# Seven block products for the gate of six experts, in place of eight, in an adaLN block of attention and a mixture of experts

## The reference, cut to what matters

```python
h = layernorm(x) * (1 + cb) + sb
weights = router(h)                               # (b, t, 8)
gate = einsum('btd,edf->ebtf', h, Wg)             # 8 experts, d = 256, f = 256
up   = einsum('btd,edf->ebtf', h, Wu)
gate[:2] += einsum('btd,edr,erf->ebtf', h, Ga, Gb)   # r = 64, same for up and down
mid = silu(gate) * up
out = einsum('ebtf,efd->ebtd', mid, Wd)
x = x + gb * einsum('bte,ebtd->btd', weights, out)
```

## Time and profile before

| | |
|---|---|
| median of three runs (lowest, highest) | 808.05 us (807.27, 809.63) |
| the profiled execution, and its span | 808.01 us, 806.3 us |
| PE, PE's weight loads, DVE, ACT, POOL busy in the span | 795.3, 710.1, 507.5, 462.2, 395.0 us |
| HBM traffic over the span | 26 GB/s |

### The profile page before, as it was taken

One profiled execution on the slowest core, in us unless ns is written; L12 is line 12 of the kernel. 1 busy time (PEld: TensorE's weight loads), 2 busy tenths in 40 slices (PEclk: granted clock), 3 DMA queues, 4 the chain that ended last, 5 costly groups with the idle time before them and its releaser, 6 DMA issues.

```text
span 806.3 us, 14755 instructions
## 1 busy us (share of the span) xinstructions
PE 795.3 (99%) x5116; PEld 710.1 (88%) x5116; DVE 507.5 (63%) x1074; ACT 462.2 (57%) x1255; POOL 395.0 (49%) x543
## 2 busy tenths in 40 slices
PE   9899999999999999999999999999999999999997
PEld 8688898999999999999999999899888888888887
DVE  5677676476476566557557658667785454454575
ACT  5777686677577677667767776643343232332322
POOL 3777587486576667567567656120011010110493
PEclk9999999999999999999999999999999999999999
DMA  9200010000000000000000000203010110100002
GB/s 333 103 28 2 1 61 1 1 8 2 0 8 2 1 7 2 2 2 6 1 1 8 1 2 2 79 1 94 38 40 2 40 40 1 40 0 1 1 1 105
DMA packets 8170, 21.53 MB, mean 27 GB/s; under 512 B 1561, under 2 KB 4249, under 8 KB 7969
## 3 DMA queue, kind: packets, MB, share of 16 engines
q1 hardware_dynamic: 7520, 20.51, 7.5%
q10 hardware_dynamic: 576, 0.08, 0.1%
HBM read 18.48 MB, written 2.11 MB: 26 GB/s over the span
## 4 chain that ended last, share of the span: by engine, by line
PE 93%; DVE 2%; POOL 1%; ACT 1%; issue 1%; DMA 1%; ACTq 0%; DVEq 0%; POOLq 0%
PE ps_o L663 14%; PE ps_proj L540 9%; PE ps_proj L542 9%; PE ps_proj L541 9%; PE ps_s L540 7%; PE ps_s L541 7%; PE ps_s L542 7%; PE ps_turn L592 4%; PE ps_y L540 4%; PE ps_y L541 4%; PE ps_y L542 4%; PE ps_turn L610 3%; PE ps_turn L540 2%; PE ps_turn L541 2%; PE ps_turn L542 2%; PE ps_o L542 2%
## 5 line engine op out<-in xcount | busy, mean ns | idle before, releaser
L663 PE MATMUL ps_o<-vaug,probs 128*128 128x129 f32 x1024 | 135.3, 275 | 1.6 <-POOL probs L1654 0.9
L663 PEld LDWEIGHTS ps_o<-vaug,probs 128*128 128x128 f32 x1024 | 129.1, 191 | 8.0 <-POOL probs L1654 1.4
L984 ACT ACTIVATE ps_s<-ps_s,knorm 128x512 f32<-128x512 f32 x128 | 79.1, 657 | 95.7 <-PE ps_s L542 95.5
L1267 DVE RECIPROCAL rden<-ps_o 128x2 f32<-128x2 f32 x128 | 21.8, 170 | 154.0 <-PE ps_o L663 153.9
L1660 POOL TENSOR_TENSOR we_lo<-raw_e,we_hi 128x512 fp32r<-128x512 f32 x22 | 28.4, 1316 | 182.3 <-ACT we_hi L1027 182.3
L1237 DVE TENSOR_TENSOR prod<-ps_proj,cs 128x1024 f32<-128x1024 f32 x76 | 92.5, 1217 | 10.9 <-ACT sq L927 10.9
L1605 POOL TENSOR_TENSOR root<-ssq,powers 128x4 f32<-128x4 f32 x76 | 77.7, 1023 | 27.6 <-ACT sq L927 27.6
L927 ACT ACTIVATE sq<-ps_proj 128x128 f32<-128x128 f32 x304 | 79.9, 278 | 18.2 <-PE ps_proj L542 15.2
L1621 POOL TENSOR_TENSOR prod<-prod 128x512 f32<-128x512 f32 x62 | 80.0, 1290 | 9.9 <-DVE prod L1237 9.9
L540 PE MATMUL ps_proj<-w_hi,h_hi 128*128 128x512 f32 x192 | 83.1, 433 | 0.9 <-DVE w_lo L1180 0.5
L1652 POOL TENSOR_SCALAR_AFFINE_SELECT probs<-probs 128x256 f32<-128x256 f32 x64 | 26.3, 410 | 106.1 <-ACT probs L992 105.8
(11 more groups left out here) (212 smaller groups left out, 2178.1 us busy)
## 6 DMA issues: line engine op xcount, KB each, us to landing
raw_e<-in_we SPq DMA_DIRECT2D x8, 768.0 KB, 4.3
raw_p<-in_wqkv SPq DMA_DIRECT2D x6, 512.0 KB, 8.1
raw_e<-in_wo SPq DMA_DIRECT2D x4, 512.0 KB, 11.6
x_all<-in_x SPq DMA_DIRECT2D x1, 1536.0 KB, 7.0
out<-acc SPq DMA_DIRECT2D x3, 512.0 KB, 2.6
x_all<-in_wmod SPq DMA_DIRECT2D x1, 1024.0 KB, 10.0
gates_a<-gate_rows_dram SPq DMA_DIRECT2D x8, 128.0 KB, 2.9
gates_b<-gate_rows_dram SPq DMA_DIRECT2D x1, 1024.0 KB, 8.0
```

What stands on the lines that cost most here:

```text
L663: mm = pe.matmul(ps_o[:, h * (D + 1):(h + 1) * (D + 1)], probs[:, s % 2, at:at + P], vaug[b % 2][:, k, i // 2, :], start=(h == 0 and k == ...
L984: act.activation(ps_s[:, t, :], ps_s[:, t, :], ACT.Tanh, scale=knorm[:, b % 2, t, i // 2:i // 2 + 1]).then_inc(tanh_done, 1)
```

## The change

For tiles 8 to 31 (`SEVEN = FIRST_OF[2]`) the gate is a 2 x 2 block product: weights A (k by f, blocks of 128 x 128) and tokens B (k by two halves of 256 tokens). In place of eight block products it takes seven, of sums of blocks, in Winograd's form of Strassen's method.

- The sums. POOL makes T1, T2, T3 and -T4 from h2 for each group n (`sums_t`, in place, once), and S1 to S4 from each expert's gate weights (`sums_s`, in place, four 128 x 128 operations, each waiting for the one before). Both are split again: ACT `round_t`, `round_s`; POOL `rest_t`, `rest_s`. `sums_s` comes between `split_e(e, 0)` and `split_e(e, 1)` in POOL's order, `rest_s` after `split_e(e, 2)`; on ACT `round_s` follows the three splits.
- PE per tile: `seven_first(m)` (A11·B11, S2·T2 in one bank, S1·T1, S3·T3 in the other, 12 matmuls of 256 columns), `up_alone(m)` (12 of 512), `down(2m-2)`, `seven_last(m)` (three products, 9 of 256, added on top), `down(2m-1)`. The gate has ps_proj only, up has ps_s only.
- The results are put together outside of PE: ACT `copy_seven` copies both banks to `seven` before `seven_last` adds to them; POOL `sums_seven` makes two sums of 256 columns and from them the last quarter of the gate (semaphores `u_made`, `pair_made`, `last_quarter`); DVE `add_quarters` adds the first of these to the second bank (two quarters, `quarters_added`); ACT `silu_seven` takes the first quarter from PSUM and the other three from SBUF in one instruction of 768 columns.
- Moved: POOL's `rest_of_output(0..3)` goes from behind the loop into it, at the end of m = 25, 26, 27, 28, `last_part(0..2)` to the end of m = 29, 30, 31. The low-rank steps come at m = 5, 6 and 7 (two each) in place of m = 5, 6, 8 and 9.
- Low rank: the factors are loaded twice, on partitions 0 to 63 and 64 to 127 (four DMAs in place of two). `lowA_both` holds A's hi part above its lo part, so that one fp32r matmul over 128 partitions gives (hi + lo)·hi, and a second over 64 gives hi·lo: four matmuls for a step in place of two float32 ones of four records.
- h2 of batches 4 and 5 is kept in DRAM (two DMAs that ACT issues in `h2_head`) and read back by SP after expert 3's weights. SP's load of an expert also waits for `s_split`, since the sums are made in the raw weights. Two scratch tiles of the router move.

```diff
-LOW_STEPS = {NEXT + 1: [0, 1], NEXT + 2: [2], NEXT + 4: [3], NEXT + 5: [4, 5]}
+LOW_STEPS = {NEXT + 1: [0, 1], NEXT + 2: [2, 3], NEXT + 3: [4, 5]}
+SEVEN = FIRST_OF[NL]
...
+            def seven_first(m):
+                e, n = TILES[m]
+                q = m - SEVEN
+                of = blocks(m)
+                if m == FIRST_OF[e]:
+                    pe.wait_ge(we_split, 3 * e - 1)
+                    pe.wait_ge(s_split, e - NL + 1)
+                if m == FIRST_OF[NL] + n:
+                    pe.wait_ge(t_split, 2 * n + 2)
+                if q:
+                    pe.wait_ge(quarter_silu, 2 * q - 1)
+                else:
+                    pe.wait_ge(mid_done, 2 * SEVEN)
+                product_of(ps_proj[:, 0, 0:S], of["A11"], of["B11"], True)
+                product_of(ps_proj[:, 0, S:], of["S2"], of["T2"], False).then_inc(seven_ready, 1)
+                if q:
+                    pe.wait_ge(quarters_added, q)
+                product_of(ps_proj[:, 1, 0:S], of["S1"], of["T1"], True)
+                product_of(ps_proj[:, 1, S:], of["S3"], of["T3"], False).then_inc(seven_ready, 1)
+            def seven_last(m):
+                pe.wait_ge(seven_copied, 2 * q + 1)
+                product_of(ps_proj[:, 0, 0:S], of["A12"], of["B21"], False).then_inc(gu_ready, 1)
+                pe.wait_ge(seven_copied, 2 * q + 2)
+                product_of(ps_proj[:, 1, 0:S], of["S4"], of["B22"], False)
+                product_of(ps_proj[:, 1, S:], of["A22"], of["-T4"], False).then_inc(gu_ready, 1)
+            def up_alone(m):
...
+                for f in range(2):
+                    pe.wait_ge(mid_done, 2 * SEVEN if m == SEVEN else 2 * m - 1 + f)
...
-                    mm = pe.matmul((ps_y[:], ps_turn[:, 0, :])[i % 2][:, k * F:(k + 1) * F], lowA[:, e, m3, k * P:(k + 1) * P],
-                                   lowB[:, e, m3, :], start=(k == 0), stop=True, skip_group_check=True)
+                    pe.matmul(dst, lowA_both[:, e, m3, at], lowB_hi[:, e, m3, :], start=(k == 0), stop=False, skip_group_check=True)
+                    mm = pe.matmul(dst, lowA_both[0:R, e, m3, at], lowB_lo[0:R, e, m3, :], start=False, stop=True, skip_group_check=True)
...
+            for m in range(SEVEN, len(TILES)):
+                seven_first(m)
+                up_alone(m)
+                down(2 * m - 2)
+                seven_last(m)
+                down(2 * m - 1)
...
+            def copy_seven(m):
+                q = m - SEVEN
+                if q == 0:
+                    act.wait_ge(low_ready, 3 * NL)
+                else:
+                    act.wait_ge(last_quarter, q)
+                    act.wait_ge(quarters_added, q)
+                for bank in range(2):
+                    act.wait_ge(seven_ready, 2 * q + bank + 1)
+                    act.activation(seven[:, 2 * bank:2 * bank + 2, :].rearrange("p a n -> p (a n)"), ps_proj[:, bank, :], ACT.Copy).then_inc(seven_copied, 1)
+            def silu_seven(m):
+                act.wait_ge(mid_done, 2 * m)
+                act.wait_ge(gu_ready, 4 * m + 3)
+                act.activation(silu[:, 0, 0:S], ps_proj[:, 0, 0:S], ACT.Silu).then_inc(quarter_silu, 1)
+                act.wait_ge(last_quarter, q + 1)
+                act.wait_ge(quarters_added, q + 1)
+                others = silu[:].rearrange("p f n -> p (f n)")[:, S:]
+                act.activation(others, others, ACT.Silu).then_inc(quarter_silu, 1)
...
+            for m in range(SEVEN, len(TILES)):
+                copy_seven(m)
+                silu_seven(m)
+                mid_head(2 * m)
+                mid_head(2 * m + 1)
+                if m == SEVEN:
+                    round_t(3)
                 for e, m3 in EXPERT_STEPS.get(m, ()):
                     split_e(e, m3)
+                    if m3 == 2:
+                        round_s(e)
...
+            for m in range(SEVEN, len(TILES)):
+                accumulate(2 * m - 2)
+                add_quarters(m)
+                for g in (2 * m, 2 * m + 1):
+                    product_seven(g)
+                for g in (2 * m, 2 * m + 1):
+                    mid_tail(g)
+                accumulate(2 * m - 1)
...
+            def sums_seven(m):
+                q = m - SEVEN
+                pool.wait_ge(seven_copied, 2 * q + 1)
+                pool.tensor_tensor(seven[:, 0, :], seven[:, 0, :], seven[:, 1, :], ALU.add).then_inc(u_made, 1)
+                pool.wait_ge(seven_copied, 2 * q + 2)
+                pool.tensor_tensor(seven[:, 2, :], seven[:, 2, :], seven[:, 3, :], ALU.add).then_inc(pair_made, 1)
+                pool.wait_ge(u_made, q + 1)
+                pool.wait_ge(pair_made, q + 1)
+                pool.wait_ge(mid_done, 2 * m)
+                pool.tensor_tensor(silu[:, 1, S:], seven[:, 0, :], seven[:, 2, :], ALU.add).then_inc(last_quarter, 1)
...
-            for m in range(NEXT, len(TILES)):
+            sums_t(0)
+            sums_t(1)
+            low_rest(0)
+            rest_t(0)
+            low_rest(1)
+            rest_t(1)
+            split_e(NL, 0)
+            sums_s(NL)
+            split_e(NL, 1)
+            sums_t(2)
+            rest_s(NL)
+            rest_t(2)
+            split_e(NL, 2)
+            for m in range(SEVEN, len(TILES)):
+                sums_seven(m)
+                if m == SEVEN:
+                    sums_t(3)
+                if m == SEVEN + 1:
+                    rest_t(3)
                 for e, m3 in EXPERT_STEPS.get(m, ()):
                     split_e(e, m3)
-            for n in range(LATE):
-                rest_of_output(n)
-            rest_of_output(LATE)
-            for n in range(LATE):
-                last_part(n)
+                    if m3 == 0:
+                        sums_s(e)
+                    if m3 == 2:
+                        rest_s(e)
+                n = m - (len(TILES) - 7)
+                if 0 <= n < LATE + 1:
+                    rest_of_output(n)
+                elif n > LATE:
+                    last_part(n - LATE - 1)
```

More of the change, by code:

```diff
@@ L380, in build @@
         low_in = sem("low_in")
+        h2_kept = [sem("h2_kept0"), sem("h2_kept1")]
+        h2_back_in = sem("h2_back_in")
+        t_made = sem("t_made")
+        t_hi_done = sem("t_hi_done")
+        t_split = sem("t_split")
+        s_made = sem("s_made")
+        s_hi_done = sem("s_hi_done")
+        s_split = sem("s_split")
+        seven_ready = sem("seven_ready")
+        seven_copied = sem("seven_copied")
+        u_made = sem("u_made")
+        pair_made = sem("pair_made")
+        last_quarter = sem("last_quarter")
+        quarters_added = sem("quarters_added")
+        quarter_silu = sem("quarter_silu")
+        low_rounded = sem("low_rounded")
+        low_split = sem("low_split")
         out_done = sem("out_done")
@@ L525, in _ @@
                 sp.wait_ge(we_split, 3 * (e - 1) - 2)
+                if e - 2 >= NL:
+                    sp.wait_ge(s_split, e - 2 - NL + 1)
                 expert(e)
+                if e == 3:
+                    sp.wait_ge(h2_turned, B)
+                    sp.wait_ge(y_gated, B)
+                    sp.dma_start(h2_back[:], h2_dram).then_inc(h2_back_in, 16)
             for n in range(LATE):
@@ L837, in _ @@
                 slot(s)
-            for m in range(NEXT, len(TILES)):
+            for m in range(NEXT, SEVEN):
                 up(2 * m)
@@ L1144, in _ @@
                     modulate2(B - 1)
+                    low_round(0)
+                    round_t(0)
+                if m == NEXT + 1:
+                    low_round(1)
+                    round_t(1)
+                if m == NEXT + 2:
+                    for m3 in range(2):
+                        split_e(NL, m3)
+                    round_s(NL)
+                if m == NEXT + 3:
+                    round_t(2)
+                    split_e(NL, 2)
[6 more added lines that the diff above has]
+                    round_t(3)
                 for e, m3 in EXPERT_STEPS.get(m, ()):
                     split_e(e, m3)
+                    if m3 == 2:
+                        round_s(e)
         @block.vector
@@ L1338, in split_first, with add_quarters, product_seven @@
                 dve.tensor_tensor(we_lo[0][:, sl, :], raw_e[:, 0, sl, :], we_hi[0][:, sl, :], ALU.subtract).then_inc(we_first, 1)
+            def add_quarters(m):
+                q = m - SEVEN
+                dve.wait_ge(gu_ready, 4 * m + 4)
+                dve.wait_ge(u_made, q + 1)
+                dve.wait_ge(mid_done, 2 * m)
+                dve.tensor_tensor(silu[:].rearrange("p f (a n) -> p (f a) n", a=2)[:, 1:3, :], ps_proj[:, 1, :].rearrange("p (a n) -> p a n", a=2),
+                                  seven[:, 0:1, :].broadcast_to([P, 2, S]), ALU.add).then_inc(quarters_added, 1)
+            def product_seven(g):
+                m, f = divmod(g, 2)
+                dve.wait_ge(quarter_silu, 2 * (m - SEVEN) + 2)
+                dve.wait_ge(mid_split, g - 1)
```

(1 more changed line is left out.)

128 lines of the change are left out of this document (118 added, 10 removed).

## The result

The changed kernel takes 860.4 us (857.76 to 861.93, six runs), the kernel before 808.02 in the same comparison: ratio 1.0643, 95% interval 1.0624 to 1.0661. Forecast were 849.4 us in 830 to 862. The profiled execution has a span of 858.0 us, against 847.7 of the sum. The time is inside the range, near its upper edge.

A forecast was written before the change was run, and what follows sets the result against it. TensorE, busy 99% of the span, was taken as the bound. 806.3 - 5.6 - 3.0 + 2.9 + 3.4 + 19.4 + 24.3 = 847.7 us of span, with 1.7 outside it 849.4 us; range 830 to 862.

The forecast's parts named there:

- part 1: Gate's matmuls: 12 of 512 columns become 21 of 256, saving 0.235 us a tile, 5.6 us over 24 tiles.
- part 2: Chain of hand-overs in an ordinary tile: no stall, 8.05 us a tile, up_alone's product with 0.27 us to spare.
- the rival that every tile stalls: Ordinary tiles also stall, 0.5 us for 14 tiles: 7 us more, 856 us; chance 0.12.
- part 3: GpSimd's queue ahead of sums_seven(m+1): expert splits cost 19.4 us, output's work moved into the loop 24.3 us.
- step 29: Silu of tile 29 to the next tile's, with one last_part addition ahead of GpSimd's sums: 8.25 us, 0.2 over.
- cheap sums: Rival: GpSimd's small sums run at their lower bounds, giving 831 us; chance 0.10.
- no loss: Rival "not slower": GpSimd's queue between sums_seven(m) and (m+1) is done by 8.98 us, leaving 805.7; chance 0.07.
- part 4: Ends of the expert stage: low rank -3.0 us, before tile 8 +2.9 us, after the last tile +3.4 us.
- four single-pass matmuls are 0.47: Low-rank step on PE: 0.47 us in place of 0.96, six steps saving 3.0 us.
- Hidden by 2.5 us: Low-rank factors' loading and splitting: done at 571.3 us, PE asks at 573.85, so no wait.
- down(14) then waits ... 1.9: Before tile 8, PE's down(14) waits 1.9 us for accumulate(12), which stands behind the router's pieces.
- The clock as a rival: PE granted 1.2 GHz after pauses: 2.6 us on last matmuls, some 1.7 in each of four splits, about 858; chance 0.09.

The follow-up runs named there:

- experiment 3: Changed kernel with the next expert's weights rounded before silu_seven and the output's GpSimd work moved to later tiles in pieces: 825.02 us.
- experiment 6: Changed kernel with GpSimd's subtraction rest_s(e) done twice for experts 3 to 7, same values: 869.46 us.
- experiment 5: Changed kernel with each low-rank step's two 128-row matmuls first, then its two 64-row ones, in place of alternating: 858.15 us.
- experiment 4: Changed kernel with low-rank factors in float32 as before (two DMAs, no low_round, no low_rest), steps at their new places: 856.46 us.
- experiment 7: Changed kernel with GpSimd waiting before rest_t(2) until VectorE has done all of the router's pieces: 854.85 us.
- experiments 2: Changed kernel with only the output's GpSimd work (rest_of_output, last_part) moved one to three tiles later, in pieces: 847.67 us.
- experiment 8: Changed kernel with early expert splits, output's work spread, float32 low rank as before and GpSimd waiting for the router, all together: 816.52 us.

## Why the prediction was right, and where it was 11 us short

The mechanism was right and it made most of the loss. That the time lies in the range owes something to luck: 12.0 us were missed in one place, and an error of 2.6 us went the other way.

**Gate, part 1: right in the pace, low in the sum.** Priced at 0.235 us a tile; measured 8.09 us for 8.31. The pace of 256-column matmuls stayed at 0.118 us. But the sum took 0.235 off each tile as if all were 8.3 us long. From the first silu of tile 8 to that of tile 31 the kernel before took 196.45 us (595.52 to 791.97); less three low-rank steps of 0.96 that is 8.42 us a tile. So the 5.6 us of the sum are 2.6 too few, and this hid a part of the loss below.

**Ordinary tile, part 2: right.** 8.05 forecast, 8.05 to 8.12 measured (7.98 to 8.00 right behind a long step). The 0.27 us to spare held; the rival that every tile stalls fell.

**GpSimd's queue, part 3: right, shown.** Additions of 256 columns took 0.73 to 0.77 us and of 128 0.46, for 0.74 and 0.47. Steps of 12.90, 18.01 and 12.00 for 13.15, 18.8 and 12.5, over the undisturbed tile 19.2 us for the 19.4 of the splits and 23.5 for the 24.3 of the output (1.8 of these are the half clock's, see step 29 below). Order alone takes 35.4 us away (experiment 3), a doubled instruction adds its length (experiment 6). The rivals of cheap sums and of no loss fell.

**The end: right.** 3.1 us of wait for 3.4, and 1.1 us more for the last matmuls at half clock, which only the rival had priced.

**Ahead of tile 8, part 4: the step that failed.** Its items lead to the first 768-wide silu at 604.3 us. It started at 616.28, 12.0 late, while the steps after it sum to within 2 us of the forecast's (230.6 us for 228.9). These 12 us, by the timelines:

- "four single-pass matmuls are 0.47": a step took 1.2 us, since the matmuls alternate between 128 and 64 rows. 6 x 0.73 = 4.4 us. What was priced as a gain of 3.0 was a loss of 1.4. That the alternation sets the pace is shown by experiment 5; its 2.6 us reached the kernel only in part.
- "Hidden by 2.5 us": the factors were in fact there in time. What wasn't there was a place for the second step: its bank is free when VectorE has read the logits, and that stood behind a `mid_lo` pair of 3.20 us and an `h_lo` of 2.28 us, beside GpSimd's `rest_t(0)` and factor subtractions (571.21 to 578.62 us). PE waited 3.0 us. The prediction named no one who waits for VectorE there, and put that wait at nothing. Shown by experiment 4 for all but 0.8 us.
- "down(14) then waits ... 1.9": 3.9 us, since eight of the router's small operations took 0.46 to 1.00 us each, for 0.16 to 0.19. Shown by experiment 7.
- The clock: 0.50, its 1.2 GHz level, behind both pauses (windows of the changed kernel: stretch, length, PE busy and count, PEclk, DMA):

```profile
572.00:574.00 2.00, 2.00 (x13) 1.00 0.00 0
574.00:576.00 2.00, 0.10 (x1) 0.86 0.00 0
576.00:578.00 2.00, 0.91 (x2) 0.50 0.01 4
...
582.00:584.00 2.00, 2.00 (x10) 0.93 0.00 0
...
608.00:610.00 2.00, 0.00 (x0) 0.90 0.84 335
...
612.00:614.00 2.00, 2.00 (x12) 0.50 0.00 0
```

At half rate PE lost 2.6 us from 577.1 to 582.3 and 2.1 us from 610.65 to the end of `seven_last(8)`.

Sum 4.4 + 3.0 + 2.0 + 2.6 + 2.1 = 14.1; less 0.9 for a wait ahead of `seven_first(8)` that didn't occur, and 0.9 by which this execution was ahead at 559 us: 12.3 of 12.0. These 12.0 us and the 1.8 by which the steps are over the forecast's, less the 2.6 of part 1, are 11.2; the profiled span was 10.3 us over the sum.

**The clock as a rival: half right.** It had a chance of 0.09 and said 858 us, nearer to the measured 860.4 than the forecast was, partly by luck. Of the four splits that it priced at 1.7 us each only one was followed by the half clock (PEclk 0.50 from 685 to 688 us, the step of 9.60 us from tile 15 to 16, 1.5 us over the others); behind the pauses at tiles 10, 18 and 22 the clock stayed at 1.00. At the end it was 1.1 us for 2.6. In the output stretch (0.50 at 788 to 792 and 800 to 811 us) it costs little, since PE has to wait there anyway. The largest part, 2.6 and 2.1 us, lay ahead of tile 8, where neither the rival nor the forecast had it.

**Step 29** took 10.03 us for 8.25. The granted clock was 0.51, 0.50 and 0.50 in the three windows from 828 to 834 us, and the silu that ends the step waited, by way of VectorE's `add_quarters`, for PE's `seven_last` and not for GpSimd (whose sums were done 2.1 us before that silu). So by the trace these 1.8 us are the half clock's too, behind a pause of 1.9 us. In experiments 2 and 3, with the output's work spread, step 29 was 8.32 us.

## What to carry to other kernels

An engine that idles is not free to use once its result is on the path: what counts is what stands ahead of the new instruction in that engine's queue at that moment, and what that work waits for. Here PE saved 0.2 to 0.3 us a tile, 5 to 7 us in 24 tiles, and the order of GpSimd's and ScalarE's work around them lost 35.4 us (experiment 3). When work is moved between queues, place each piece where its inputs are long ready and its user is far, and look on PE's other suppliers for what slows down beside it. And before small matmuls are rewritten, price them from rows with the same row counts in the same alternation.

## What the runs showed of the hardware

**Some VectorE operations are held by a running GpSimd instruction.** `TENSOR_TENSOR`, `SCALAR_TENSOR_TENSOR` and `TENSOR_SCALAR` operations on SBUF ended with GpSimd's instruction, to 0.05 us (experiment 7 shows two), and long ones on both sides stretched (experiment 3). Not all operations on SBUF did: in the changed kernel `TENSOR_REDUCE` (0.19 us at 597.11 and 604.12) and `RECIPROCAL` (0.18 us at 605.35) ran while a GpSimd instruction was under way and kept their time. The kernel before already had it, one row that I passed over; DVE, then POOL timeline:

```profile
595.01 1.23 DVE L1443 SCALAR_TENSOR_TENSOR r_c<-r_a,r_fb 128x32 f32<-128x32 f32 x1
```

```profile
594.90 1.30 POOL L1660 TENSOR_TENSOR we_lo<-raw_e,we_hi 128x512 fp32r<-128x512 f32 x1 [7.96 <-ACT we_hi L1027]
```

An operation of 32 columns took 1.23 us and ended at 596.24, GpSimd's at 596.20. Products and accumulations that read PSUM kept their 0.69 and 0.87 us throughout.
The Trainium skill says it ("GPSIMD Engine Reference", Key points): GpSimd shares its SBUF interfaces with VectorE, and instructions of VectorE with two SBUF inputs or in a two-port mode contend. The traces agree, and give a size that those points don't: up to the whole rest of GpSimd's instruction.

**Row counts.** Matmuls of 256 columns that alternate between 128 and 64 rows start 0.31 us apart, for 0.118 with one row count.

**The clock.** In experiment 8 the granted clock fell to about 0.5 behind a pause of 0.8 us amid low-rank steps, and in experiment 4 it stayed at 1.00 behind the same pause. Why isn't settled here, nor why the clock fell behind the pauses at tile 14 of the changed kernel and not behind those at tiles 10, 18 and 22.
